# A two-layer decoder's expert stage: two batches routed at once, its weights loaded one stage earlier

## What is computed

```
h      = x @ Wr + br ; h[:] += BONUS            # 8 router logits a row
gates  = softmax(h)                              # over 8
top, i = the 2 largest gates and their numbers   # then share = top / sum(top)
hid    = relu(x @ Wd + bd)                       # 8 experts x 16
y      = sum over the 2 chosen e of share_e * (hid_e @ Wu_e + bu_e)
out    = layernorm(x + y)                        # (r - mean) / sqrt(var + 1e-5)
```

## Time and profile before

| | |
|---|---|
| time, median of 3 runs | 2038.38 us (2033.85 to 2040.03) |
| the profiled execution: span from first to last instruction | 2041.2 us |
| TensorE busy | 1832.9 us, 90% |
| VectorE busy | 1253.9 us, 61% |
| ScalarE busy | 918.1 us, 45% |
| GpSimd busy | 290.8 us, 14% |
| mean granted TensorE clock | 0.958 |
| last barrier | about 1952.7 us, so the last stage takes 88.5 us |

### The profile page before, as it was taken

How to read it: one execution, slowest core, us unless ns; L and a number is a source line. 1 busy time by engine, 2 the same in 40 slices (tenths; PEclk the granted TensorE clock), 3 DMA queues, 4 the chain that set the end, 5 groups by cost and what they waited for, 6 DMA issues and landing times. The chain is left out here.

```text
span 2041.2 us, 33020 instructions
## 1 busy us (share of the span) xinstructions
PE 1832.9 (90%) x12272; PEld 1493.2 (73%) x12272; DVE 1253.9 (61%) x2330; ACT 918.1 (45%) x2376; POOL 290.8 (14%) x347
## 2 busy tenths in 40 slices
PE   6979999999997889999999987899997698889966
PEld 5868999999885778888888885677775455555543
DVE  3446444444447656555654536788887587778847
ACT  2225333333334443333333214676666587778811
POOL 0000000000012111111111001333334112111001
PEclk9989999999999999999999998999997899899988
DMA  3022000000014221101110013000013575665134
GB/s 106 32 95 92 21 22 22 22 21 1 22 53 129 83 73 42 47 19 40 48 37 17 11 42 124 12 32 32 32 53 96 148 170 147 151 150 127 49 118 142
DMA packets 86253, 136.62 MB, mean 67 GB/s; under 512 B 9480, under 2 KB 25480, under 8 KB 86096
## 3 DMA queue, kind: packets, MB, share of 16 engines
q1 hardware_dynamic: 86096, 134.52, 23.2%
HBM read 79.88 MB, written 21.05 MB: 49 GB/s over the span
## 5 line engine op out<-in xcount | busy, mean ns | idle before, releaser
L2224 ACT ACTIVATE e_p<-e_s_ps,e_nb 128x512 f32<-128x512 f32 x256 | 175.1, 698 | 45.5 <-DVE e_nb L2270 43.7
L2270 DVE TENSOR_REDUCE e_nb<-e_s_ps 128x2 f32<-128x1024 f32 x128 | 155.8, 1218 | 51.2 <-PE e_s_ps L2346 50.5
L1710 ACT ACTIVATE p<-p,nb,rq 128x128 f32<-128x128 f32 (+1 forms) x256 | 136.9, 541 | 92.9 <-DVE nb L1811 92.9
L2356 PE MATMUL e_t_ps<-ident,e_p 128*128 128x128 f32 x1024 | 147.7, 283 | 21.2 <-DVE e_pT L2277 13.5
L894 PE MATMUL yp<-ccy,toep 128*128 128x288 f32 x600 | 159.1, 413 | 5.7 <-ACT ccy L876 3.6
L2356 PEld LDWEIGHTS e_t_ps<-ident,e_p 128*128 128x128 f32 x1024 | 120.1, 146 | 58.9 <-issue 49.6
L80 PE MATMUL q_ps<-a_xt_hi,wq_hi 128*128 128x256 f32 x512 | 151.3, 296 | 4.1 <-DVE wo_lo L112 4.1
L1231 DVE SCALAR_TENSOR_TENSOR hm<-gu_ps,us_col,sg 128x256 f32<-128x256 f32 x88 | 42.3, 481 | 177.4 <-ACT sg L1120 177.4
L82 PE MATMUL q_ps<-a_xt_hi,wq_lo 128*128 128x256 f32 x512 | 145.7, 285 | 0.0
L81 PE MATMUL q_ps<-a_xt_lo,wq_hi 128*128 128x256 f32 x512 | 145.4, 284 | 0.0
L527 ACT ACTIVATE ex<-ex 128x512 f32<-128x512 f32 x64 | 40.4, 632 | 213.1 <-DVE ex L590 213.1
(11 more groups left out here) (300 smaller groups left out, 5151.7 us busy)
## 6 DMA issues: line engine op xcount, KB each, us to landing
x_after<-n_r SPq DMA_DIRECT2D x24, 512.0 KB, 3.0
toep<-padded_kernels SPq DMA_DIRECT2D x32, 256.0 KB, 3.6
qs<-e_xh SPq DMA_DIRECT2D x64, 128.0 KB, 2.5
qs<-e_xl SPq DMA_DIRECT2D x64, 128.0 KB, 2.6
ks<-e_ch SPq DMA_DIRECT2D x64, 128.0 KB, 2.6
ks<-e_cl SPq DMA_DIRECT2D x64, 128.0 KB, 2.7
x<-x_after SPq DMA_DIRECT2D x12, 512.0 KB, 4.5
x<-in_x SPq DMA_DIRECT2D x8, 512.0 KB, 4.0
```

Source lines behind the costliest of these rows:

```text
L1710: act.activation(p[n % 3][:, h, part[t]], p[n % 3][:, h, part[t]], ACT.Exp, bias=nb[i][:, t, h:h + 1], scale=rq[u][:, t:t + 1], accum_out= ...
L2224: act.activation(pr[i][:, a, :], s_ps[i][:, a, :], ACT.Exp, bias=nb[i][:, a:a + 1], accum_out=sums[t][:, j, q:q + 1]).then_inc(e_done, 1)
L2270: dve.tensor_reduce(nb[i][:], s_ps[i][:], AX.X, ALU.max, negate=True).then_inc(nb_done, 1)
L2356: last = pe.transpose(t_ps[a][:, k, :], pr[m % 2][:, a, k * P:(k + 1) * P], core.ident[:])
```

## The change

- Weights: `load_weights` is issued by `l1_cross`'s SyncE in the body of b = 1, between `residual(2)` and `norm.store(0)`. It is eight transfers: router weights (16 KB), down weights (256 KB), two bias rows (4 KB and 64 KB), up weights (256 KB) and `bu` three times (16 KB each, to partitions 0, 32 and 64). They go into the free part of the ring buffer. GpSimd clears `bu_rows` at the head of `l1_cross`.
- x: `l1_cross` loads batches 0 and 1 of the next stage (at b = 6 and b = 7, each behind a store). `l1_experts` issues the other six at its start. Each batch has a buffer of its own; the second copy `xr` is gone.
- Pairs: shift, route and the turning of hidden values run on 4 tiles of 128 rows (PAIR = 4) at once, four times in place of eight.
- The residual is added in place into the batch's own buffer. Nothing waits for a store any more, except the end.
- The norm is applied by ScalarE as Identity with bias and scale columns, which GpSimd computes with four small instructions a batch where there were two.
- The bias product: the weights are split into a rounded part and a rest, both fp32r, in one 128-deep tile `parts` (columns 0 to 7 and 64 to 71 the rounded part, 32 to 39 the rest), against `bup`, which holds rounded `bu` at rows 0 and 32 and its rest at row 64. So it is one fp32r product instead of one f32 product.

```diff
 # l1_cross, SyncE
+                    if b == 1:
+                        after.load_weights(sp)
                     if not (ints(b) and b == 0):
                         norm.store(sp, b - 1)
+                    if b >= B - EARLY:
+                        sp.wait_ge(norm.stored, 16 * (b - B + EARLY + 1))
+                        after.load(sp, b - B + EARLY)
-                after.load_x(sp)
 # l1_cross, GpSimd
+                after.clear(pool)
 # l1_experts, SyncE
+                for b in range(EARLY, B):
+                    ahead.load(sp, b)
+                for b in range(B):
+                    sp.wait_ge(y_done, T * b + T)
+                    sp.dma_start(rows(y, b), xs[b][:]).then_inc(stored, 16)
 # GpSimd, batch b
+                    pool.tensor_tensor(rstd[u][:], mv[u][:, :, 1], core.eps[:], ALU.add).then_inc(ve_done, 1)
+                    pool.tensor_tensor(shiftby[u][:], mv[u][:, :, 0], minus_one[:], ALU.mult).then_inc(ve_done, 1)
+                    pool.tensor_tensor(rstd[u][:], rstd[u][:], core.minus_half[:], ALU.pow).then_inc(rstd_done, 1)
+                    pool.tensor_tensor(shiftby[u][:], shiftby[u][:], rstd[u][:], ALU.mult).then_inc(shift_done, 1)
 # ScalarE
+                def apply(b):
+                        act.activation(xs[b][:, t, :], xs[b][:, t, :], ACT.Identity, bias=shiftby[u][:, t:t + 1],
+                                       scale=rstd[u][:, t:t + 1]).then_inc(y_done, 1)
+                turned(0)
+                turned(1)
+                act.activation(bup[:], ahead.bu_rows, ACT.Copy).then_inc(bup_hi, 1)
+                for n in range(N):
+                    if n + 1 < N:
+                        turned(2 * n + 2)
+                    exponential(n)
+                    if n + 1 < N:
+                        turned(2 * n + 3)
+                    if n >= 2:
+                        apply(2 * n - 4)
+                        apply(2 * n - 3)
+                    hidden(n)
+                for b in range(B - 4, B):
+                    apply(b)
 # VectorE, end of route(n): two more instructions, and the order
+                    dve.tensor_copy(hi, w[:].unsqueeze(2).to_broadcast([P, PAIR, 2, E])).then_inc(parts_done, 1)
+                    dve.tensor_tensor(parts[:, :, 32:32 + E].bitcast(F32R), w[:], parts[:, :, 0:E], ALU.subtract)
+                for n in range(N):
+                    if n:
+                        residual(2 * n - 2)
+                        residual(2 * n - 1)
+                    shift(n)
+                    route(n)
+                    if n:
+                        statistics(2 * n - 2)
+                        statistics(2 * n - 1)
+                for b in (B - 2, B - 1):
+                    residual(b)
+                    statistics(b)
 # TensorE; project(b) waits for lh_done n = b // 2, as one h_ps serves all pairs
+                turn_x(0)
+                turn_x(1)
+                project(0)
+                project(1)
+                for n in range(N):
+                    if n + 1 < N:
+                        for b in (2 * n + 2, 2 * n + 3):
+                            turn_x(b)
+                            project(b)
+                    turn_hidden(n)
+                    out(n)
```

More of the change, by code:

```diff
@@ L2426, in l1_experts @@
         pb = lambda n, s: ctx.enter_context(nc.psum_tensor(n, s, F32))
[L2427 to L2430, removed]
+        wrd, wu, bias = ahead.wrd, ahead.wu, ahead.bias
+        bup = sb("f_bup", [P, D], F32R)
         numbers = sb("f_numbers", [P, 1, 1, E])
-        xs = [core.x0, sb("f_x1", [P, T, D])]
-        xr = [sb(f"f_xr{u}", [P, T, D]) for u in range(2)]
+        minus_one = sb("f_minus_one", [P, T])
@@ L2434, in l1_experts @@
+        for b in range(EARLY, B):
+            ahead.xs.append(sb(f"f_x{b}", [P, T, D]))
+        xs = ahead.xs
         xT = [sb(f"f_xT{u}", [P, KT, S]) for u in range(2)]
[L2435 to L2441, removed]
@@ L2464, in _ @@
             def _(sp):
[L2465 to L2491, removed]
+                for b in range(EARLY, B):
+                    ahead.load(sp, b)
                 for b in range(B):
-                    body(b, b % 2, b < B - 3)
@@ L2600, in body @@
-                def body(b, u, first, second):
-                    shift(b, u)
-                    if not first and not second:
-                        norm.apply(dve, b - 2)
-                    route(b)
-                    if not first:
-                        residual(b - 1, 1 - u)
-                dve.wait_ge(w_loaded, 64)
-                dve.tensor_scalar(bias[:, 0, 0:E], bias[:, 0, 0:E], BONUS, None, ALU.add).then_inc(prepared, 1)
-                dve.wait_ge(prepared, 3)
-                def tail(b, u):
-                    norm.apply(dve, b - 2)
-                    residual(b - 1, 1 - u)
-                    norm.apply(dve, b - 1)
@@ L2650, in out @@
-                def out(b, u):
-                    pe.wait_ge(hT_done, 2 * b + 2)
-                    for t in range(T):
-                        if t == 0:
-                            wait_from(pe, norm.added, T * b)
-                        pe.matmul(o_ps[t][:], hwT[:, t * P:(t + 1) * P], wu[:], start=True, stop=False)
-                        pe.matmul(o_ps[t][:], wT[:, t * P:(t + 1) * P], bup[:],
-                                  start=False, stop=True).then_inc(o_mm, 1)
-                def body(b, u, first, last):
-                    if not last:
-                        turn_x(b + 1, 1 - u)
-                    if not first:
-                        turn_hidden(b - 1)
-                    if not last:
-                        project(b + 1, 1 - u)
-                    if not first:
-                        out(b - 1, 1 - u)
@@ new lines, in out @@
+                def out(n):
+                    pe.wait_ge(hT_done, 2 * n + 2)
+                    for i in range(PAIR):
+                        if PAIR * n + i >= T:
+                            pe.wait_ge(added, PAIR * n + i - T + 1)
+                        ts = slice(i * P, (i + 1) * P)
+                        pe.matmul(o_ps[i % T][:], hwT[:, ts], wu, start=True, stop=False)
+                        pe.matmul(o_ps[i % T][:], pT[:, ts], bup[:], start=False, stop=True).then_inc(o_mm, 1)
+                turn_x(0)
```

291 lines of the change are left out of this document (184 added, 107 removed).

## The result

Median over nine runs each: 2027.10 us after (2022.97 to 2032.67), 2039.14 us before on the same chip; the ratio is 0.9947 with a 95% interval of 0.9933 to 0.9961, so 8 to 14 us faster, all of it beyond the 6.1 us (0.3%) that the prediction takes as the least that can be told. Forecast: 2031.7. The profiled executions span 2041.2 us before and 2029.4 after.

What follows compares the result with a forecast made beforehand. In the expert stage VectorE's work and the store wait were taken to bound, with TensorE bounding pairs afterwards; -12.2 us there plus 5.5 in cross attention gave -6.7, from 2038.4 to 2031.7, range 2026 to 2038.

Steps and rivals of the forecast that it cites:

- rival 1: Cross attention: small transfers fill gaps, store delayed 2.0 us instead of 5.5; about 11 us gained, 2027.5; chance 0.20.
- The expert stage: Last stage: early weights, pairs on TensorE and the end summed to a gain of 12.2 us, bounds 7 to 16.
- The first shift: Expert stage: first shift 8.7 us behind the stage's start, where it was 11.8.
- TensorE's last wait: Expert stage, last pair: TensorE waits 6.5 us for add, shift, exponential and route, and its clock falls.
- The tail: Expert stage's end: GpSimd 1.08 us plus 0.5 for two new instructions, then apply 1.4.
- about 7.9 us a batch: Expert stage before: VectorE's need per batch for shift and bias, route, add, statistics and apply.
- Rivals 3 and 4: Expert stage: 3, VectorE stays the bound, 2039.9, chance 0.06; 4, TensorE's clock stays half, about 2052 over two pairs, chance 0.06.
- the eight transfers: Cross attention: weight and bias loads queued ahead of the first store delay it 5.5 us, bounds 2.7 and 9.
- rival 2: Cross attention: the weights hold the store up by 9 us; 3.2 us gained, 2035.2; chance 0.18.
- the lower bound of 2.7: Cross attention: least store delay in us, from the bytes, 0.63 MB more.
- all of it is on the path: Cross attention: the whole 5.5 us store delay lengthens the run, and later batches do not make up for it.
- a delay of 7 or more: Cross attention: skill-based estimate, 4.5 us for six transfers of 64 KB or less beside 2 to 3 for two large ones.

Runs made afterwards that it cites:

- run 3: Changed kernel with the bias product in plain f32 again, without splitting; median 2039.64 us, ratio 1.0009 to the kernel before, expert stage 85.4 us.
- run 9: Changed kernel, pairs kept, with the norm applied by VectorE again instead of ScalarE; ratio 0.9944 to the kernel before, expert stage 75.4 us.
- run 8: Changed kernel with both x of the next pair turned ahead of both projections; ratio 0.9941 to the kernel before, expert stage 74.5 us.
- run 4: Kernel before with eight residual buffers in the expert stage, so no residual waits for a store; median 2030.26 us, ratio 0.9967.
- run 5: Changed kernel with eight further 16 KB transfers ahead of cross attention's first store; executed once, cross attention 356.4 us.
- run 6: Changed kernel with two further 512 KB transfers ahead of cross attention's first store; executed once, cross attention 356.5 us.
- run 11: Changed kernel with two result buffers in cross attention's norm and expert x of batch 1 loaded later; median 2010.48 us, ratio 0.9873 to the kernel before.
- run 12: Changed kernel routing one batch at a time, plus two result buffers in cross attention's norm; median 1999.38 us, ratio 0.9826 to the kernel before.

## Why the prediction was right, and where it was not

**The time is in the stated range of 2026 to 2038, in part because that range is wide.** 2027.10 lies just outside the forecast's own 2027.5 to 2035.5, and on rival 1's 2027.5. Of the signs named ahead, those of the expert stage came true, and the one of the transfers came out as rival 1's: VectorE idle 5.58 us (under 6, where the forecast had about 9), and the expert stage starting at 1953.8 instead of about 1958. So the expert stage was forecast, and cross attention was not.

**The expert stage: -12.8 us, forecast -12.2.** The terms held one by one. The first shift came 8.9 us after the stage's start (forecast 8.7), a pair is 14.13 us (14.16), the fp32r products are 0.23 apart in steady work (0.24), TensorE's last wait is 6.23 (6.5) and falls into half clock as said. The steady state was TensorE's by a little; runs 3 and 9 show it (extra work on TensorE costs 2.5 us a pair, extra work on VectorE nothing), and run 8 that VectorE is 0.5 behind. The tail from GpSimd's first instruction (2023.35) to the end of the two applications (2026.29) is 2.9 us, 1.08 + 0.5 + 1.4 in the sum. One term of the kernel before was short: the prediction says that VectorE needs about 7.9 us a batch, but its five parts add up to 7.7; run 4 has 7.80 with 0.34 idle in it. Rivals 3 and 4 are out: the clock is 1.00 from 1962.5 to 2007 in spite of three waits a pair.

**The step that failed is the eight transfers: +5.5 us was put for a store's delay that is 1.7 us at the store, about 1 in TensorE's waits, and not to be told from zero in the stage's length.** Two things were wrong in it. Its size: I added issue time to a busy queue, with the 6.15 us of the bias row as support, but that row's time is most likely waiting behind others (argued from the landing times above, not tested), and the store waits behind the same others anyway. The eight issues took 4.9 us (4.1 in the prediction), and still the store landed only 1.7 later. Runs 5 and 6 separate the two: eight issues cost 0.7 us, a megabyte over 5. Even the lower bound of 2.7, from the bytes alone, is above the 1.7 measured. Rival 1 had this mechanism, with 2.0; rival 2, with 9, is out. And its reach: "all of it is on the path" did not hold. Cross attention with the weights ahead of the store took 349.3, 352.3, 354.3, 355.6, 356.0 and 356.4 us, without them ahead of it 352.0, 354.2, 354.6 and 355.4. Both means are 354.0. The reason is in the traces: in all fourteen executions the stage's length is TensorE's busy time, plus its waits for this add, plus 37.9 to 39.0 us. The waits sum to 14.8 to 15.3 us with the weights ahead of the store and to 13.6 to 14.5 without, means of 15.0 and 14.0, so 1.0 us reaches TensorE. The busy time, for the same 2368 products, runs from 295.9 to 303.2 us in these ten: how much of it is at half clock moves the stage by more than the weights do.

With the DMA engines already busy, eight transfers of 16 KB cost 0.7 us together (run 5). The Trainium skill (DMA: Bandwidth & Descriptors, Bandwidth) holds transfers under 64 KB to be descriptor-dominated, which had given a delay of 7 or more; the delay is 1.7, so here, queued behind larger ones, they did not cost what that estimate gave them. The applications with two column operands are longer than the prediction took: 0.73 us was put for one and 1.4 for two, and the trace has 797 to 814 ns for one and 1.52 us for the last two. The Trainium skill (ScalarE: Activation LUTs, What ACT_TABLE_LOAD costs) had led to an estimate of 799 ns; the trace agrees, with a median of 805.

The median lies 4.6 us under the forecast. Between the two profiled executions the span fell by 11.8 us, where 6.7 were forecast: 4.5 of the difference are cross attention (1.0 longer instead of 5.5) and 0.6 the expert stage. That cross attention is just 1.0 longer in these two is partly luck, as it differs by up to 7 us between executions of the same instructions.

**What the prediction didn't ask: the parts.** The change's parts are not worth what their place in its name suggests. Within the expert stage the bias product is worth 9.7 us, the early weights 3.1, the norm on ScalarE nothing, freeing the store's wait 5.7 (in the kernel before), and the pairing, with the order of work that goes with it, costs 6.3. I computed pairs only against the old kernel, never against the same edits without pairing, and so took an edit that loses as the heart of one that gains.

## What to carry over

- Work out a batched version against the unbatched one with all the other edits in. Widening small instructions relieves the engine that runs them; here the other engine bounded, its waits for copies came with the pairs, and the pipeline filled in units of a pair. Both cost more than was saved.
- A transfer put ahead of one that is waited for cost its bytes here, and not its issue or its landing time in a busy queue; a megabyte cost more for its size than the 0.66 MB of weights. Better to take away the wait: a second buffer was worth some 16 us, the order of the queue 1.7 at most.
- Where executions of one kernel scatter, cut the traces at fixed marks and compare stages.

## What the runs showed of the hardware

A short stall is not always over when it ends. In cross attention TensorE stood 5.05 us up to 1691.54, and over the next 10 us its clock was at 0.72; in the execution of run 3, with the same instructions there, it stood 4.75 us and the clock was then at 0.85. A later batch took 43.4 us with the clock at 0.91 (1770.24 to 1813.61, changed kernel) and 41.0 at 1.00 (1765.81 to 1806.79, run 3), and TensorE stood 3.2 us in it in both. So a stall of the same length costs half clock behind it in one execution and not in another.

I had put a stall at its length. Against run 11, where only 2.6 us of these waits are left, the executions with 13.6 to 15.3 us of them had 3.8 to 11.1 us more busy time for the same products (10.4 in the changed kernel). That is the 7 us scatter of the stage. In run 11 the clock was 1.00 from 1680 to 1900, and four runs lay within 2.4 us. But this doesn't explain all of the scatter of 10 to 16 us between the runs of one kernel: run 12 has the same 1.00 in that stretch, and its five runs still lie 8.5 us apart, for a reason that wasn't sought.
